# Context sums of a phase-mixer layer: fp32 adds on VectorE and accumulating DMAs in place of 64 fp16 token-sum products on TensorE

## The reference, cut to what matters

```python
cm_real = x * cos_phi
cm_imag = x * sin_phi
mem_real = jnp.cumsum(cm_real, axis=1) / position
mem_imag = jnp.cumsum(cm_imag, axis=1) / position
ret_real = mem_real * cos_phi + mem_imag * sin_phi
ret_imag = mem_imag * cos_phi - mem_real * sin_phi
context = jnp.concatenate([cm_real, cm_imag, ret_real, ret_imag], axis=-1)
h = _layernorm(context, ln_gamma, ln_beta)
h = jnp.einsum('bsd,ed->bse', h, W1) + b1
h = jax.nn.gelu(h, approximate=False)
h = jnp.einsum('bsd,ed->bse', h, W2) + b2
return x + h
```

## Time and profile before

| | |
|---|---|
| median of 3 runs | 1599.02 us (1599.0 to 1600.2) |
| the profiled execution, its own time | 1598.85 us |
| its span | 1597.1 us, 30622 instructions |
| TensorE busy (PE) | 1524.3 us, 95% |
| VectorE busy (DVE) | 1418.5 us, 89% |
| ScalarE busy (ACT) | 1268.4 us, 79% |
| GpSimd busy (POOL) | 505.0 us, 32% |

### The profile page before, as it was taken

The page is one execution under the profiler, slowest core; times in us unless marked ns, Lnnn a source line. Parts: engine busy times, 40 slices in busy tenths (PEclk is TensorE's granted clock), DMA queues, the critical chain, the costliest instruction groups (busy, mean ns, idle before and its releaser), DMA issues.

```text
span 1597.1 us, 30622 instructions
## 1 busy us (share of the span) xinstructions
PE 1524.3 (95%) x11177; PEld 932.7 (58%) x11177; DVE 1418.5 (89%) x2304; ACT 1268.4 (79%) x1805; POOL 505.0 (32%) x331
## 2 busy tenths in 40 slices
PE   3789999999999999999999999999999999999994
PEld 2455556666655666665566666556666556666662
DVE  7999999999999999999998999999999999999832
ACT  6768878888987888897788788878888887887743
POOL 1222333323233333223333322333332233333310
PEclk9799999999999999999999999999999999999997
DMA  5212332332333333233233323323323332332313
GB/s 204 54 40 57 77 70 63 69 79 53 67 80 67 67 67 80 54 67 80 63 68 70 67 68 67 80 54 74 73 59 75 67 80 54 73 61 56 65 27 53
DMA packets 135300, 109.73 MB, mean 69 GB/s; under 512 B 74992, under 2 KB 125424, under 8 KB 135152
## 3 DMA queue, kind: packets, MB, share of 16 engines
q0 software_dynamic: 26112, 50.34, 18.7%
q1 hardware_dynamic: 107408, 53.77, 11.8%
q10 hardware_dynamic: 1632, 3.67, 0.6%
HBM read 23.87 MB, written 33.55 MB: 36 GB/s over the span
## 4 chain that ended last, share of the span: by engine, by line
PE 57%; DVE 22%; issue 9%; ACT 9%; SPq 1%; DMA 1%; DVEq 0%; POOL 0%; POOLq 0%; ACTq 0%
PE ps L881 16%; PE ps L896 11%; PE ps L912 11%; PE ps L931 10%; PE ps L841 5%; DVE mr L1161 4%; DVE ph L1119 3%; ACT base L549 2%; DVE arena L1226 2%; ACT xs L566 2%; DVE bn L1245 2%; DVE mi L1180 1%; SPq L440 1%; DVE rows L1262 1%; DVE rr L1192 1%
## 5 line engine op out<-in xcount | busy, mean ns | idle before, releaser
L881 PE MATMUL ps<-arena,w_hi 128*128 128x512 f16 x2048 | 610.0, 379 | 1.6 <-DVE arena L1202 1.4
L881 PE MATMUL ps<-arena,w_lo 128*128 128x512 f16 x1024 | 388.6, 379 | 0.0
L881 PEld LDWEIGHTS ps<-arena,w_hi 128*128 128x128 f16 x2048 | 198.2, 98 | 223.3 <-issue 3.2
L896 PE MATMUL ps<-turned,fw_t 128*128 128x512 f16 x1024 | 257.7, 381 | 20.1 <-DMA turned<-rows 16.8
L912 PE MATMUL ps<-fw_t,arena 128*128 128x256 f16 x2048 | 254.9, 273 | 0.4 <-DVE arena L1270 0.4
L912 PEld LDWEIGHTS ps<-fw_t,arena 128*128 128x128 f16 x2048 | 200.2, 98 | 57.6 <-issue 5.9
L504 POOL TENSOR_TENSOR sqr<-sqr,turn 128x1024 f32<-128x1024 f32 x32 | 88.3, 2760 | 379.4 <-ACT sqr L613 365.1
L660 ACT ACTIVATE arena<-ps,relu_bias,relu_scale 128x512 f32<-128x512 f32 x256 | 191.9, 773 | 13.8 <-PE ps L896 13.4
L1270 DVE TENSOR_TENSOR arena<-arena 128x512 f16<-128x512 f32 x256 | 170.8, 688 | 28.4 <-ACT arena L669 22.4
L931 PE MATMUL ps<-w_hi,arena 128*128 128x256 f16 x1024 | 183.4, 273 | 0.0
L881 PEld LDWEIGHTS ps<-arena,w_lo 128*128 128x128 f16 x1024 | 100.2, 98 | 121.2 <-issue 0.7
(11 more groups left out here) (192 smaller groups left out, 2894.8 us busy)
## 6 DMA issues: line engine op xcount, KB each, us to landing
x_rows<-in_L_attn_x SPq DMA_DIRECT2D x32, 512.0 KB, 4.2
rr<-qa POOLq DMA_DIRECT2D x32, 512.0 KB, 4.5
ri<-qb POOLq DMA_DIRECT2D x32, 512.0 KB, 4.4
out<-x SPq DMA_DIRECT2D x32, 512.0 KB, 2.9
out<-x POOLq DMA_DIRECT2D x32, 512.0 KB, 6.2
arena<-in_L_attn_W ACTq DMA_DIRECT2D x1, 2048.0 KB, 11.0
arena<-in_L_ffn_W SPq DMA_DIRECT2D x2, 1024.0 KB, 11.3
turned<-rows SPq DMA_TRANSPOSE x128, 2.4
```

What stands on the lines that cost most here:

```text
L881: last = pe.matmul(ps[:, 4 + m], w[:, k, m * P:(m + 1) * P], a[:, c.b, k], start=(i == 0), stop=(i == len(passes) - 1))
L896: last = pe.matmul(ps[:, 4 + m % KE], fw1_t[:, k, m * P:(m + 1) * P], a[:, k], start=(i == 0), stop=(i == len(passes) - 1))
```

## The change

The four parts are added in fp32 before TensorE sees them. VectorE writes `cmr + cmi` into `cs`, the cosine's buffer, which has been read by then (`context_pair`, 1024 elements a partition). Two more DMAs from GpSimd's queue add `rr` and then `ri` to it, the second only after the first has landed (`context_sums`). In the next step VectorE adds the two channel blocks into `ctx_sum`, the second half of `sqr` (`context_sum`, 512 elements). `context_stats` then takes 4 fp32 products of one column for the sum and 4 for the squares, straight from fp32, so that `sums_hi` and `square_lo` go. It waits for `ctx_sum` and `q_done`. The cosine of the next chunk waits until `ctx_sum` has been made. GpSimd's product L519 gets one more wait, for the running sums of the real part (`sumr_done`). The four semaphores each of `f1`, `relu`, `rh`, `rl` and `f2` become one each, with the same conditions; those one-line edits are left out below.

```diff
@@ -160,9 +160,7 @@
         qb = sb("qb", [P, KD, CH])
         sqr = sb("sqr", [P, KD, CH])
         rb = sb("rb", [P, CH])
-
-        q_hi = sqr[:, 1, 0:CH // 2].bitcast(F16)
-        q_lo = sqr[:, 1, CH // 2:CH].bitcast(F16)
+        ctx_sum = sqr[:, 1]
         ones_h = sb("ones_h", [P, P], F16)
         turned2 = sb("turned2", [P, 2, KD, CH], F16)
         h2, l2 = turned2[:, 0], turned2[:, 1]
...
@@ -344,9 +343,9 @@
             wait(eng, turned2_done, c.counts.value(16 * NT, 16 * NT * (c.more + 1 - back)))
-        def need_block(eng, sems, m, c, back=0):
-
-            wait(eng, sems[m % SLOTS], c.counts.value(2, 2 * (c.more - back) + m // SLOTS + 1))
+        def need_block(eng, s, m, c, back=0):
+
+            wait(eng, s, c.counts.value(KF, KF * (c.more - back) + m + 1))
         def stand_alone(eng):
@@ -486,8 +485,6 @@
                     inverse_std_2(now)
                 if before:
                     output_sum(before)
-                if nxt:
-                    square_lo(nxt, ahead)
                 if far:
                     inverse_std_1(far)
                 if nxt:
@@ -495,6 +492,7 @@
                 if ahead:
                     product_imag_sin(ahead)
                     retrieve(ahead)
+                    context_sums(ahead)
                     square_sums(ahead)
             def square_sums(c):
@@ -505,16 +503,18 @@
                 need(pool, q2_done, c)
                 pool.tensor_tensor(sqr[:, 0], sqr[:, 0], sqr[:, 1], ALU.add).then_inc(q_done, 1)
-            def square_lo(c, after):
-                if after:
-                    need(pool, frac_done, after)
-                need(pool, q_done, c)
-                need(pool, qh_done, c)
-                pool.tensor_tensor(q_lo, sqr[:, 0], q_hi, ALU.subtract).then_inc(ql_done, 1)
+            def context_sums(c):
+                need(pool, pair_done, c)
+                need_sum(pool, rr_done, c)
+                pool.dma_start(cs[:, :, :], rr[:, :, :], accum_op=ALU.add).then_inc(pair_r_done, 16)
+                need_sum(pool, pair_r_done, c)
+                need_sum(pool, ri_done, c)
+                pool.dma_start(cs[:, :, :], ri[:, :, :], accum_op=ALU.add).then_inc(pair_i_done, 16)
             def product_imag_sin(c):
                 need(pool, mi_done, c)
                 need(pool, sin_done, c)
+                need(pool, sumr_done, c)
                 need_sum(pool, rr_done, c, 1)
                 pool.tensor_tensor(qa[:, :, :], mi[:, :, :], sn[:, :, :], ALU.mult).then_inc(qa_done, 1)
@@ -527,6 +527,7 @@
             inverse_std_1(second)
             product_imag_sin(first)
             retrieve(first)
+            context_sums(first)
             square_sums(first)
             prepared(pool)
             run(pool, step, -1)
@@ -588,6 +589,7 @@
                 need(act, frac_done, c)
                 act.activation(turn[:, :, :], ph[:, :, :], ACT.Abs).then_inc(abs_done, 1)
                 need(act, abs_done, c)
+                need(act, ctx_sum_done, c, 1)
                 act.activation(cs[:, :, :], turn[:, :, :], ACT.Sin, scale=-TWO_PI,
                                bias=half_pi[:, 0:1]).then_inc(cos_done, 1)
@@ -611,10 +613,6 @@
                 need(act, mr_done, c)
                 need(act, stats_done, c, 1)
                 act.activation(sqr[:, :, :], mr[:, :, :], ACT.Square, scale=SQUARE_SCALE).then_inc(sqr_done, 1)
-
-            def sums_hi(c):
-                need(act, q_done, c)
-                act.copy(q_hi, sqr[:, 0]).then_inc(qh_done, 1)
             def square_imag(c):
                 need(act, mi_done, c)
@@ -658,7 +656,7 @@
                 else:
                     need_block(act, rl_done, m + SLOTS, c, 1)
                 act.activation(rf[:, m % SLOTS], ps[:, 4 + m % KE], ACT.Relu, scale=relu_scale[:, 0:1],
-                               bias=relu_bias[:, m:m + 1]).then_inc(relu_done[m % SLOTS], 1)
+                               bias=relu_bias[:, m:m + 1]).then_inc(relu_done, 1)
             def relu_hi(c, m):
                 need_block(act, relu_done, m, c)
@@ -666,12 +664,10 @@
                     need_block(act, f2_done, m - SLOTS, c)
                 else:
                     need_block(act, f2_done, m + SLOTS, c, 1)
-                act.copy(rh[:, m % SLOTS], rf[:, m % SLOTS]).then_inc(rh_done[m % SLOTS], 1)
+                act.copy(rh[:, m % SLOTS], rf[:, m % SLOTS]).then_inc(rh_done, 1)
             def step(s):
                 before, now, nxt, ahead, far = s.chunk(-1), s.chunk(0), s.chunk(1), s.chunk(2), s.chunk(3)
-                if nxt:
-                    sums_hi(nxt)
                 if before:
                     output(before)
                 if ahead:
@@ -843,22 +839,15 @@
                 last.then_inc(omega_done, 1)
             def context_stats(c, after):
-                for part in range(4):
-                    need(pe, ch_done[part], c)
-                    need(pe, cl_done[part], c)
                 if after:
                     need(pe, u_done, after)
+                need(pe, ctx_sum_done, c)
                 for j in range(NT):
-                    halves = [(a, k) for k in range(KC) for a in (ch, cl)]
-                    for i, (a, k) in enumerate(halves):
-                        pe.matmul(ps[:, 3, j:j + 1], a[:, c.b, k, j * P:(j + 1) * P], ones_h[:, 0:1],
-                                  start=(i == 0), stop=(i == len(halves) - 1))
-                need(pe, qh_done, c)
-                need(pe, ql_done, c)
+                    pe.matmul(ps[:, 3, j:j + 1], ctx_sum[:, j * P:(j + 1) * P], ones[:, 0:1], start=True, stop=True)
+                need(pe, q_done, c)
                 for j in range(NT):
-                    for src in (q_hi, q_lo):
-                        last = pe.matmul(ps[:, 3, NT + j:NT + j + 1], src[:, j * P:(j + 1) * P], ones_h[:, 0:1],
-                                         start=(src is q_hi), stop=(src is q_lo))
+                    last = pe.matmul(ps[:, 3, NT + j:NT + j + 1], sqr[:, 0, j * P:(j + 1) * P], ones[:, 0:1],
+                                     start=True, stop=True)
                 last.then_inc(stats_done, 1)
             def spread(c):
...
@@ -1202,6 +1191,18 @@
                 dve.tensor_tensor(cl[:, c.b, 2 * part:2 * part + 2], src, ch[:, c.b, 2 * part:2 * part + 2],
                                   ALU.subtract).then_inc(cl_done[part], 1)
+            def context_pair(c):
+                need(dve, cmr_done, c)
+                need(dve, cmi_done, c)
+                need(dve, ra_done, c)
+                need(dve, rb_done, c)
+                dve.tensor_tensor(cs[:, :, :], cmr[:, :, :], cmi[:, :, :], ALU.add).then_inc(pair_done, 1)
+
+            def context_sum(c):
+                need_sum(dve, pair_i_done, c)
+                need(dve, q_done, c)
+                dve.tensor_tensor(ctx_sum, cs[:, 0], cs[:, 1], ALU.add).then_inc(ctx_sum_done, 1)
+
             def context_variance(c):
                 need(dve, stats_done, c)
                 dve.tensor_scalar(cmu[:, :], ps[:, 3, 0:NT], 1.0 / (RSTD_SCALE * C), None, ALU.mult).then_inc(cmu_done, 1)
@@ -1268,12 +1269,14 @@
                 else:
                     need_block(dve, f2_done, m + SLOTS, c, 1)
                 dve.tensor_tensor(rl[:, m % SLOTS], rf[:, m % SLOTS], rh[:, m % SLOTS], ALU.subtract)\
-                   .then_inc(rl_done[m % SLOTS], 1)
+                   .then_inc(rl_done, 1)
             def step(s):
                 now, nxt, ahead, far = s.chunk(0), s.chunk(1), s.chunk(2), s.chunk(3)
                 if now:
                     lean_2(now)
+                if nxt:
+                    context_sum(nxt)
                 if ahead:
                     fraction(ahead)
                 if far:
@@ -1317,6 +1320,7 @@
                     relu_lo(now, 0)
                 if ahead:
                     product_real_sin(ahead)
+                    context_pair(ahead)
                 if now:
                     relu_lo(now, 1)
                     relu_lo(now, 2)
@@ -1464,6 +1468,7 @@
             retrieve_real_cos(first)
             retrieve_imag_cos(first)
             product_real_sin(first)
+            context_pair(first)
             context_lo(first, 0, cmr[:, :, :])
             first_lo(second)
             dve.wait_ge(p_spread, 3)
```

17 lines of the change are left out of this document (9 added, 8 removed).

## The result

The changed kernel takes **1603.53 us** (median of 8 runs, 1602.76 to 1604.59); the kernel before, run beside it, 1599.55 us. The ratio is **1.0026, interval 1.0015 to 1.0037**: slower by a quarter of a per cent, where 1585.5 was forecast and 1600 was the upper end of the range.

What follows compares the result with a forecast made beforehand. TensorE was taken to set the pace, with the rows' loop almost as long. On 1598.85 us: -6.9 (slack), -6.7 (block 3's bank), -0.6 (last step), +0.8 (preparation) = -13.4, so 1585.5 us; range 1580 to 1600.

Steps and rivals of the forecast that it cites:

- rows' loop: From omega's end, other engines make the transposed rows, landing 0.49 us before TensorE needs them; the change would not shorten it.
- The token sums on TensorE: 8 fp32 products at 1.2 us replace 72 at 1.80, shortening TensorE's list by 0.6 us a step, bounds 0.0 to 1.4.
- How much of it counts: Of TensorE's 0.6 us saving, only the slack before the transposed rows counts: 0.3 in 23 steps, 6.9 us.
- Block 3's bank: TensorE's ffn_in gaps of 0.16 and 0.30 us close as VectorE reads block 3 earlier: 0.23 x 29 steps, 6.7 us.
- `context_pair`: VectorE's second half: 1.3 us gained ahead of block 3's scale_hidden, 1.13 given back by this add, so about even.
- four signs: Late fraction (over 6.9 us after omega); relu_lo or context_lo over 2 us; TensorE waiting for ctx_sum; xl not waiting for ScalarE.
- slow rival: GpSimd's sum of squares starts before VectorE's last relu_lo and holds it: 2.6 us x 29, about 1661; within a 0.18 chance.
- The rival with costly fp32 products: On TensorE, fp32 products cost 0.2 us each, as much as those replaced; only block 3's gap closes: about 1592, chance 0.20.
- The DMAs: Two more 0.5 MB issues on GpSimd's queue, landing after 4.5 us each, cost nothing; cover 10 us.
- The preparation: The pair's 1.13 us stand ahead of the context_lo TensorE waits for, partly regained in the first step: plus 0.8 us.
- 0.4 us of waiting left for `xh`: VectorE would still wait 0.4 us for ScalarE, keeping its last relu_lo ahead of GpSimd's sum of squares.
- GpSimd in the way or another wait of that kind: The slower outcome, with GpSimd or a similar wait holding up the step: from 1603 us up, chance 0.18.

Runs made afterwards that it cites:

- e2: The kernel before with one edit: GpSimd's product_imag_sin also waits for sumr_done, no sum moved; 1590.02 us, ratio 0.9943.
- e1: The changed kernel with context_pair moved back behind the fourth relu_lo (block 3); 1597.10 us, ratio 0.9988.
- e8: e1 with context_pair moved further back, behind the low halves of x (xl); 1607.15 us, ratio 1.0047.
- e5: The changed kernel without its two accumulating DMAs, so the means are wrong; 1605.18 us, ratio 1.0035.
- e3: The changed kernel with product_imag_sin no longer waiting for sumr_done; 1625.67 us, ratio 1.0164.
- e7: e1 with the token sums' fp32 arrays split into fp16 halves (16 fp16 products) and context_sum moved ahead of the phases; 1661.20 us, ratio 1.0397.
- e4: The changed kernel with the preparation's two-column fp32 product issued six times instead of once, to shift code fetches; 1602.69 us, ratio 1.0024.
- e6: e1 with four idle fp16 one-column products (eight TensorE instructions) more in each step; 1596.60 us, ratio 0.9983.
- e9: e8 without the two accumulating DMAs, the retrieved halves left out of the sum; 1652.90 us, ratio 1.0342.

## Why the prediction was wrong

**What bounds the kernel: right.** TensorE sets the pace before and after, and the rows' loop is close behind it. That loop did not change in a running step: `context_sum` fits under the wait for the rounded phase. It takes 0.68 us at 728.58 in a step of the changed kernel and VectorE still idles 0.56 before `fraction`, against the 0.74 of the earlier trace rows. Cost nothing, as forecast. The first transposing DMA is issued 18.67 or 18.80 us after `omega`'s end, by turns, in both kernels, and an undisturbed step's rows land at 24.9 to 25.1. TensorE does not come to wait for them in nearly every step, as the forecast had it, because it hardly became shorter.

**The token sums on TensorE: the first step that failed.** I took 8 x 0.15 = 1.2 us, from the product of 2 columns in the earlier trace rows, because it was nearest in columns. Measured: 1.70. The range of 0.4 to 1.8 held it and so did the rival, whose 0.2 a product was the better row. Counting records would have told: each of the 16 costs 106 ns, and the fp32 products of 128 columns in the earlier trace rows showed 0.11 a record too. The 0.15 was one isolated product, and its start to the next start is no price for sixteen in a row. The Trainium skill's rule (TensorE: Matmul & The Clock Gate, "LDWEIGHTS" and "Weight-path perf modes": fp32 weights are loaded without the fast path, 107 ns a load) gave 1.7 us, and the trace agrees with 1.70; I had weighed it and set it aside.

**How much of it counts.** The slack of 0.3 x 23 = 6.9 us fell away with it: 0.10 in an undisturbed step, 2.8 us, of which 1.2 is left in the mean. The slower groups of transposes take the rest (0.043 a step in the mean against 0.10).

**Block 3's bank: right, 0.23 forecast and 0.22 measured (e2).** The forecast 1.3 us of lead at that point is there: the sums take 2.03 less and `memory_real` 0.74 more, and both `ffn_in` runs are at 1.89.

**`context_pair`: the step that failed and decided the sign.** "1.3 us gained ahead of `scale_hidden` of block 3, and 1.13 given back behind it. VectorE's second half is about even". The sum of the two is even, but a lead does not keep. Between the two places VectorE waits for ScalarE's `relu_hi(0)` (0.68 at 751.09), ScalarE for TensorE's `ffn_in`, and this wait absorbs the lead. The pair behind it is then a net delay for `relu_lo`, and so for `ffn_out`, 0.38 us a step or 10.6 in all, as the difference to e2. e1 and e8 show it from the other side: 21.40, 21.18, 21.02 as the pair moves back. I costed VectorE's list as a total where each `relu_lo` has a due time of its own. None of the four signs that I had set down for "wrong" appeared (`fraction` starts at 6.91 or 7.04 us, by turns, as in the kernel before): they watched the rows' loop, `ctx_sum` and the slow rival, and nothing watched `ffn_out`. The rival with costly fp32 products had their price right, and its 1592 failed by this same step.

**The DMAs: right in a running step (e5)**, with less cover than forecast: the first takes 6.0 us to land, not 4.5, and GpSimd is done with the second issue 3.6 us before its squares (763.08 and 766.70), not 7. Their effect in e8, where they keep GpSimd away from `relu_lo`, was not foreseen.

**The preparation.** `+0.8` was forecast for the pair, and the first `omega` of the table ends 0.7 later. That is no confirmation: up to 0.75 of it goes with the DMAs (e5), and the same end lies anywhere from 156.09 (e2) to 160.43 (e3) in the kernels here, e7 apart, and at 157.80 in e4. What the pair costs there is open.

**The transposing DMAs.** I called their lateness "six times in the 29 steps" and took it as given. It depends on where the fetches of TensorE's code fall, and fewer instructions move them: in the changed kernel three steps hold seven fetches, so every third step is hit. The sum of what the steps have over an undisturbed one is 3.8 us before and 5.4 after. In the steps with a fetch alone it is 2.9 and 4.9, elsewhere 0.9 and 0.5. So this costs some 1.6 us net; e6 shows it in its direction and size.

**The slow rival** did not come about in the changed kernel; its mechanism is shown by e9, as is the sums' block by e2 and e3 in both directions. The forecast's condition "0.4 us of waiting left for `xh`" held: 0.30 in the changed kernel.

Together: forecast -13.4, measured +4.8 in the spans. The difference of 18.2 is 5.7 in the first part, 11.0 in the second (6.7 forecast gained, 4.3 lost), 0.6 that the last step was to give, and the rest at the start and end. The cause of the 1.0 us after the last `omega` is open. The measured time lies in what I had given 0.18, "GpSimd in the way or another wait of that kind"; the wait that came was not one that I had named.

## What to carry to other kernels

Price a many-short-products part by its instructions, from a row with several of them in a row, not by its columns. Before you set time won on an engine against work added to it later in its list, look whether it waits for another engine in between: the lead ends at that wait, and the added work then counts in full. And try the parts of a change alone: here one added wait, meant to order two engines on a shared resource, was worth 9 us, and the rest of the change cost 13.
